# GpSimd adds pairs of probability blocks that only enter softmax sums, so that TensorE weighs one block for two; new planner constants, warm-up and last turn

## What is computed

```python
# layer 0: attention, 16 heads of 8, softmax FIRST, causal mask AFTER it
scores = einsum('bqhd,bkhd->bhqk', Q, K) / sqrt(8)
alpha = softmax(scores, axis=-1)             # sums run over all 1024 keys
alpha = where(causal, alpha, 0)              # then the later keys are dropped
x = x + einsum('bhqk,bkhd->bqhd', alpha, V)
# layers 1 and 3: 8 experts, top 2 by softmax gates (chosen with a bias), and one shared expert
# layer 2: the same attention with rotary tables, no mask, output matrix and bias
```

## Time and profile before

| | us |
|---|---|
| runs shown | 1748.45, 1748.89, 1739.39 |
| median | 1748.45 |
| the profiled execution's own time | 1754.32 |
| its span, first to last instruction | 1752.6 |

### The profile page before, as it was taken

The page is one execution under the profiler, slowest core; times in us unless marked ns, Lnnn a source line. Parts: engine busy times, 40 slices in busy tenths (PEclk is TensorE's granted clock), DMA queues, the critical chain, the costliest instruction groups (busy, mean ns, idle before and its releaser), DMA issues.

```text
span 1752.6 us, 44428 instructions
## 1 busy us (share of the span) xinstructions
PE 1710.3 (98%) x16824; PEld 866.0 (49%) x16824; DVE 1527.3 (87%) x2895; ACT 1420.8 (81%) x2840; POOL 945.8 (54%) x1397
## 2 busy tenths in 40 slices
PE   7999999999999999999999999999999999999988
PEld 3444444555545555455554545445454455555557
DVE  7888888998989989899889999889998989999727
ACT  2688887898878888688886998879997889999862
POOL 5254444566966678476772546535544364555530
PEclk7799998999989999899999999989997999999999
DMA  5211111000101001010110102010110001100000
GB/s 171 89 55 63 69 57 51 21 21 20 57 2 56 21 20 56 12 47 21 32 45 2 38 20 74 20 38 2 45 33 13 2 13 34 38 8 2 8 7 13
DMA packets 39124, 61.13 MB, mean 35 GB/s; under 512 B 5568, under 2 KB 20544, under 8 KB 38784
## 3 DMA queue, kind: packets, MB, share of 16 engines
q1 hardware_dynamic: 38880, 58.28, 10.2%
q10 hardware_dynamic: 32, 0.01, 0.0%
HBM read 29.96 MB, written 27.26 MB: 33 GB/s over the span
## 4 chain that ended last, share of the span: by engine, by line
PE 89%; DVE 6%; ACT 2%; issue 1%; POOL 1%; SPq 1%; DMA 0%; ACTq 0%; DVEq 0%; POOLq 0%
PE ps_sum L1358 29%; PE ps_banks L1324 25%; PE ps_banks L1378 13%; PE ps_banks L1399 8%; PE ps_banks L1299 4%; DVE negmax L1096 3%; PE ps_banks L1259 2%; PE ps_banks L1313 2%; PE ps_banks L1245 1%; PE ps_banks L1266 1%; PE ps_banks L1369 1%; ACT probs L908 1%; SPq L623 1%; PE ps_banks L1281 1%; PE ps_sum L1337 1%
## 5 line engine op out<-in xcount | busy, mean ns | idle before, releaser
L1096 DVE TENSOR_REDUCE negmax<-ps_banks 128x1 f32<-128x512 f32 x2048 | 1296.0, 684 | 151.7 <-PE ps_banks L1299 131.9
L908 ACT ACTIVATE probs<-ps_banks 128x512 f32<-128x512 f32 x2048 | 1099.9, 610 | 184.6 <-PE ps_banks L1324 176.0
L1299 PE MATMUL ps_banks<-kx,qx 24*128 24x512 f32 x2048 | 603.7, 512 | 6.9 <-DVE negmax L1096 2.4
L1324 PE MATMUL ps_banks<-qx,kx 26*128 26x512 f32 x2048 | 557.2, 508 | 5.8 <-ACT probs L908 3.6
L1358 PE MATMUL ps_sum<-probs,vg 128*9 128x256 f32 (+1 forms) x6144 | 425.8, 381 | 2.0 <-ACT sums L915 1.3
L1324 PEld LDWEIGHTS ps_banks<-qx,kx 26*128 26x128 f32 x2048 | 214.6, 186 | 381.5 <-ACT probs L908 129.4
L781 POOL TENSOR_TENSOR hid<-hid,first 128x512 f32<-128x512 f32 x124 | 158.2, 1276 | 210.2 <-DVE hid L1123 123.6
L1299 PEld LDWEIGHTS ps_banks<-kx,qx 24*128 24x128 f32 x2048 | 243.1, 187 | 38.9 <-DVE negmax L1096 17.6
L793 POOL TENSOR_SCALAR scaled<-scaled,gates 128x128 f32<-128x128 f32 x496 | 175.2, 371 | 80.5 <-ACT scaled L965 79.9
L755 POOL TENSOR_TENSOR pdiag<-probs,causal 128x512 f32<-128x512 f32 x128 | 163.3, 1279 | 98.9 <-ACT probs L908 64.4
L1358 PEld LDWEIGHTS ps_sum<-probs,vg 128*9 128x9 f32 x6144 | 129.0, 90 | 163.2 <-issue 71.3
(11 more groups left out here) (121 smaller groups left out, 1383.6 us busy)
## 6 DMA issues: line engine op xcount, KB each, us to landing
qk_rows<-limbs SPq DMA_DIRECT2D x36, 512.0 KB, 3.7
qx<-qk_rows SPq DMA_DIRECT2D x124, 96.0 KB
kx<-qk_rows SPq DMA_DIRECT2D x124, 96.0 KB
qx<-mlimbs SPq DMA_DIRECT2D x508, 2.0 KB
qk_rows<-prod_c SPq DMA_DIRECT2D x8, 512.0 KB, 3.4
qk_rows<-prod_s SPq DMA_DIRECT2D x4, 512.0 KB, 3.0
out_dram<-x SPq DMA_DIRECT2D x8, 256.0 KB, 2.5
x<-in_x SPq DMA_DIRECT2D x3, 512.0 KB, 6.0
```

The costliest lines, as they stand in the source:

```text
L908: act.activation(m.probs[:, blk % PROB_SLOTS, EXP_HEADS[k], :], bank, ACT.Exp, scale=SCALE).then_inc(s.freed[SCALAR], 1)
L1096: dve.tensor_reduce(m.negmax[:, unit // UNITS % 2, half, col:col + 1], bank, AX.X, ALU.max, negate=True).then_inc(s.freed[VECTOR], 1)
L1299: pe.matmul(bank_of(("scores", unit, k)), m.qx[rows, n % SLOTS, tile * P:(tile + 1) * P], m.kx[rows, n % SLOTS, half * CHUNK:(half + 1) * ...
L1324: pe.matmul(bank, m.kx[rows, n % SLOTS, j * P:(j + 1) * P], m.qx[rows, n % SLOTS, half * CHUNK:(half + 1) * CHUNK], start=True, stop=True) ...
```

## The change

Four things are done. First, in layer 0 and half 0, after the exponentials of blocks j = 5 and j = 7, GpSimd adds the block before into this one, in `m.probs`, over 128 partitions by 2048 elements; TensorE then weighs only the odd block, both parts at the second step of the block two later, after waiting for the new semaphore `paired`. The even block isn't weighed. Second, the account's constants for the banks are replaced. Third, `warm` is made of four tiles in place of two, once per step as before in the first two blocks, and it is put also after the even units from 14 to 24 of `begun`. Fourth, the last chunk's items in `ended` stand at fixed units: `turn` after unit 6 in place of 4, `logits` 7 in place of 6, the chain in units 8, 9, 10 in place of 7, 8, 9.

```diff
+WARM_FROM = 14
-READ_AFTER = 90
-WEIGHT = {"exp": (11, 49), "scores": (11, 60), "h1": (85, 100), "h3": (85, 0), "y": (95, 50), "mix": (95, 90),
-          "turn": (50, 80), "q": (95, 100), "k": (95, 100), "v": (95, 100), "direct": (190, 70), "qk": (95, 69), "logits": (95, 20),
-          "oturn": (50, 50), "omix": (100, 50), "maxima": (20, 25), "sums": (55, 50)}
-OTHER_WORK = {"weigh": (55, 0, 0), "copy": (0, 50, 0), "high": (0, 107, 0), "stats": (0, 0, 120), "moments": (0, 0, 60),
-              "combine": (0, 0, 33), "finish": (0, 0, 25), "chain": (0, 0, 20), "product": (0, 0, 69), "write": (0, 0, 70)}
+READ_AFTER = 80
+WEIGHT = {"exp": (11, 49), "scores": (18, 60), "h1": (54, 100), "h3": (85, 0), "y": (57, 50), "mix": (95, 90),
+          "turn": (50, 80), "q": (95, 64), "k": (95, 60), "v": (95, 160), "direct": (300, 110), "qk": (95, 55),
+          "logits": (95, 20), "oturn": (50, 30), "omix": (100, 50), "maxima": (20, 40), "sums": (55, 50)}
+OTHER_WORK = {"weigh": (55, 0, 0), "copy": (0, 50, 0), "high": (0, 107, 0), "stats": (0, 0, 96), "moments": (0, 0, 75),
+              "combine": (0, 0, 33), "finish": (0, 0, 25), "chain": (0, 0, 12), "product": (0, 0, 86), "write": (0, 0, 70)}
+def only_summed(blk):
+    n, half = place(blk // NT)
+    return masked_after(n) and blk % NT >= (half + 1) * CT
...
         items += both[2:]
+        if part and only_summed(blk) and blk % 2:
+            items.append(("pair", blk))
         if part and diagonal(blk):
             items.append(("mask", blk))
         if blk >= WEIGH_LAG:
+            behind = blk - WEIGH_LAG
             between = any(item[0] in BETWEEN for item in side.get(step + 1 - part, []))
-            items += [("weigh", blk - WEIGH_LAG, k) for k in (range(2 * part) if between else (part,))]
+            if not only_summed(behind):
+                items += [("weigh", behind, k) for k in (range(2 * part) if between else (part,))]
+            elif behind % 2 and part:
+                items += [("weigh", behind, k) for k in range(2)]
...
-            items.append(("warm", blk, part))
+            items.append(("warm",))
...
         plan += side.get(unit, []) + scores_of(unit)
+        if unit >= WARM_FROM and unit % 2 == 0:
+            plan.append(("warm",))
...
-    stages = [[("oturn", c)], [("omix", c), ("oadd", c)], [("stats", 3, c), ("moments", 3, c), ("apply", 3, c)],
-              [("turn", 3, c)], [("logits", 3, c)],
-              *([("chain", 3, c, 1, k) for k in range(CHAIN) if k // PART == part] for part in range(-(-CHAIN // PART)))]
-    side = {}
-    for i, stage in enumerate(stages):
-        add_side(side, {1 + i * (late - 1) // len(stages): stage})
+    side = staged(1, (0, ("oturn", c)), (1, ("omix", c)), (1, ("oadd", c)),
+                  (2, ("stats", 3, c)), (2, ("moments", 3, c)), (2, ("apply", 3, c)), (5, ("turn", 3, c)), (6, ("logits", 3, c)),
+                  *((late - 4 + k // PART, ("chain", 3, c, 1, k)) for k in range(CHAIN)))
...
+    def add_pair(blk):
+
+        pool.wait_ge(s.freed[SCALAR], counts.freed("exp", blk, GH - 1) + 1)
+        one, other = (m.probs[:, k % PROB_SLOTS, :, :].rearrange("p h q -> p (h q)") for k in (blk, blk - 1))
+        pool.tensor_tensor(one, one, other, ALU.add).then_inc(s.paired, 1)
...
-    def warm(blk, part):
+    def warm():
         pe.wait_ge(s.acc_cleared, 1)
-        for t in range(2):
+        for t in range(CT):
...
+            if only_summed(blk):
+                pe.wait_ge(s.paired, counts.nth("pair", blk) + 1)
...
         if part:
-            last.then_inc(s.weighed, 1)
+            last.then_inc(s.weighed, 2 if only_summed(blk) else 1)
```

More of the change, by code:

```diff
@@ L299, in ended @@
     late = len(units) - NE
-    assert late > 2
-    stages = [[("oturn", c)], [("omix", c), ("oadd", c)], [("stats", 3, c), ("moments", 3, c), ("apply", 3, c)],
-              [("turn", 3, c)], [("logits", 3, c)],
-              *([("chain", 3, c, 1, k) for k in range(CHAIN) if k // PART == part] for part in range(-(-CHAIN // PART)))]
-    side = {}
-    for i, stage in enumerate(stages):
-        add_side(side, {1 + i * (late - 1) // len(stages): stage})
+    assert late > 10
+    side = staged(1, (0, ("oturn", c)), (1, ("omix", c)), (1, ("oadd", c)),
+                  (2, ("stats", 3, c)), (2, ("moments", 3, c)), (2, ("apply", 3, c)), (5, ("turn", 3, c)), (6, ("logits", 3, c)),
+                  *((late - 4 + k // PART, ("chain", 3, c, 1, k)) for k in range(CHAIN)))
     items += [("h1", done), ("h3", done), ("product", done)]
@@ L515, in signals @@
     s.hidden, s.added, s.mixed = (sem(k) for k in ("hidden", "added", "mixed"))
-    s.weighted = sem("weighted")
+    s.weighted, s.paired = sem("weighted"), sem("paired")
     s.biased = sem("biased")
@@ L835, in pool_program @@
             mask(*of)
+        elif kind == "pair":
+            add_pair(*of)
         elif kind == "apply" and not by_vector(kind, *of):
@@ L1436, in tensor_program @@
         elif kind == "warm":
-            warm(*of)
+            warm()
         elif kind == "fill":
```

## The result

The kernel after takes 1820.78 us (median of 4 runs, 1818.34 to 1830.08), the kernel before 1745.73 in the same job: a ratio of 1.043, 95% interval 1.040 to 1.046. The forecast was 1775, its range ended at 1801. The profiled execution took 1818.34 us, with a span of 1816.4. Between the medians lie 75.1 us, between the two profiled spans 63.8: the profiled execution of the kernel before, 1754.32, was 8.6 us slower than its median here. First the page of after: busy time, the clock in slices, and the engines of the chain that ended last.

A forecast was written before the change was run, and what follows sets the result against it. TensorE was taken as the bound, busy 1710.3 of 1752.6 us. The terms +21.4 + 5 + 3 + 5 + 0 - 3 - 5 = +26.4 on a median of 1748.45 gave 1775 us, range 1742 to 1801.

The forecast's parts named there:

- What goes: Layer 0: 64 weighed blocks become 32, so at most 32 x 0.98 = 31.4 us go, if TensorE never waits.
- the waits: Layer 0: TensorE stands for GpSimd's adds, 25 to 60 us in all, near 7 us singly in spans 14, 22, 30.
- The clock: Behind four or five long waits, work of some 2 us runs at half rate: +5 us, ends 0 and 20.
- The adds: Layer 0: 32 GpSimd adds over 2048 columns, 4.55 us each, 146 us of GpSimd work.
- The count of the spans: Even spans 10 to 30, with expert units: net shifts of +25.4 us, less 4 for bank waits that go, +21.4.
- The rival that GpSimd's adds might be in time: Layer 0: GpSimd is let through earlier, up to 22 of 31.4 us come through, 1718 us; chance 0.12.
- the clock falls and stays down: After each long wait, half rate over 8 us or so, VectorE held: +15 and +6 more, 1796 us; chance 0.18.
- Spans without expert units: Five spans of layer 0: count gives +10.8 us, half taken because TensorE had slack, +5, ends 0 and 11.
- VectorE's holds: Spans 10, 18 and 26: GpSimd's adds hold up VectorE's chain steps, about 1 us each, +3, ends 0 and 14.
- Account: Bank choice, the only part touching layer 2: 0, ends -12 and +12; layer 2 moving over 10 us would count against the forecast.
- warm-up: At the start: more matmuls may bring the full clock rate earlier, up to -9, or cost +7; taken as -3 us.
- last turn: At the end: the 4.01 us wait for xn goes, and the slow matmuls behind it: -5 us, ends -6 and 0.

The follow-up runs named there:

- e3: The kernel after without GpSimd's adds and the wait for them, the even block of each pair not weighed: 1774.94 us, 1.014 against before.
- e2: The kernel after without the pairs (new bank account, warm-up and last turn kept, every block weighed): 1743.68 us, 1.000 against before.
- e8: The kernel after with each GpSimd add over only half of the pair's columns (1024): 1783.48 us, 1.019 against before.
- e10: The kernel after, complete, plus one fill (0.98 us of zero matmuls) where each even block was weighed: 1822.63 us, 1.040 against before.
- e15: e2 without the added warm matmuls, so with the warm-up of before: 1744.19 us, 0.999 against before.
- e1: The kernel before with the pairs alone (old bank account, warm-up and last turn): 1811.54 us, 1.037 against before.
- e16: The kernel before with the new last turn alone: 1741.31 us, 0.997 against before.
- e6: e2 with two fills of zero matmuls added per former pair, all weighings kept: 1807.97 us, 1.033 against before.
- e9: e3 with one fill of zero matmuls in place of each weighing left out: 1764.57 us, 1.008 against before.

## Why the forecast missed

Two steps failed. "What goes" put 31.4 us of TensorE's work down as time, of which under 3 came; the waits were counted too long by about as much, so that this error hardly shows in the total. The clock, put at +5, cost about 55 (an estimate, below): that is the term that took the time out of the range.

**The adds, right.** 4.53 us against 4.55; GpSimd's busy time up by 143.8 (forecast 146); in spans 14, 22 and 30 the second add starts 5.23 to 5.24 us after its data (5.4). The list between the adds is what the forecast said.

**"What goes", wrong: the step that failed first.** "TensorE is the bound there", from 99.89 of 100 busy, and so at most 31.4 us go. e3 less e2 shows under 3 us. The count of the spans then set the saved 0.98 against each wait. Rows 2 can't show a bank wait that matmuls in flight cover, and VectorE at 90.90 and ScalarE at 85.89 in that same row were the warning: three engines pass the same banks on to each other, and each bounds the others. The rival that GpSimd's adds might be in time, priced at 1718, would not have come out there even if it had been true: e8 is nearly that case, with 3.6 us of waits, and takes 1783.

**The waits, too long, and right in the net by luck.** Measured 22.8 us in 13 waits, the longest 5.3, against 25 to 60 with some near 7. Of them 15.1 fall in the spans with expert units; the count's gross waits there were 25.4 and the 22 x 0.98 it had taken off, 47. So there the waits were 32 us too long, and the saving nearly 22 too large. TensorE comes later to each wait than I had it: it saves nothing on the way, and ahead of the long wait in span 14 it was at the half rate. The net looks right because the two errors nearly cancel: after less e2, the line through the 32 spans has a slope of 0.35 and crosses zero at +0.77; the 157 us more at the half rate make 55 us of the 79.5, and the rest is 24.5, where the forecast had 21.4 and 5 for the same waits. The split is rough: the crossing has a standard error of 11 us over the 32 spans, and e10 shows that clock and waits stand in for each other. The long waits' spans do cost more than the forecast's +5.5: spans 14 and 15 together 8.2 us over e2, 22 and 23 7.3, 30 and 31 8.3, with 10.2, 6.8 and 13.7 us more at the half rate.

**The clock, wrong in kind and size.** +5 against about 55 (an estimate, from the slope above). The forecast let the clock fall behind the long waits only, and for some 2 us. In after, layer 0 has 18 stretches at the half rate, of 3.4 to 20.5 us, and some stand behind gaps of under 0.5 us: e3, where TensorE waits for no add, and e8, where it waits 3.6 us, have 109 and 106 us of layer 0 at the half rate, e2 17. Of the rivals, "the clock falls and stays down" had the direction; with its 15 us more it had 20 for the clock, over a third of what came. The Trainium skill (TensorE: Matmul & The Clock Gate, "Terms") prices throttled time at half of it; here the slope is a third, 0.31 to 0.35, as if part of a half-rate stretch were hidden behind the other engines, which is not shown by itself. By the skill's half the 157 us would be 79 (an estimate from that page), the whole of the change, and nothing would be left for the waits.

**Spans without expert units, wrong by the clock.** +5 against +29.3 (after less e2, spans 0 to 9). Their half-rate time rose by 77 us, which at 0.35 is 27; the remaining 2 is near the forecast, though 7.7 us of the waits stand there. I had called the 4 us of idle time in 100 slack. It was where the clock is nearest to its fall (0.95 in rows 2).

**VectorE's holds, the mechanism right, off the path.** The three chain steps of spans 10, 18 and 26 fell into the adds, 2294 ns for the longest of a group whose median is 208:

```profile
L1212 DVE TENSOR_TENSOR room<-rank,small x20: 179/208/2294, 341.6 to 1792.3; 128x64 f32<-128x64 f32 x12, 128x32 f32<-128x32 f32 x8
```

In spans 18 and 26 the time against e2 rose by 0.5 and 0.3 us. So of +3 most did not come.

**Account, warm-up, last turn.** The account was put at 0: e2 and e15 are at 1.000 and 0.999, so no change can be told from it. Layer 2, which only the account touches, is 9.6 us shorter in after, just short of the 10 that were to count against the forecast. That is not the account: e1, with the account of before, has 803.5 too. Over the 17 profiles with the new account, layer 2 takes 0.30 us more for each us that it has at the half rate (13.7 to 61.4 us), and none lies over 2.3 us off that line; it gives 811.2 at the 47.8 us of before and 804.0 at e1's 23.9, where 810.2 and 803.5 were measured. So the account moves layer 2 by about 1 us. The line bears out the third of a us with no pairs near. The warm-up was put at -3: the start is 5.3 us longer, and over the twelve profiles with this warm-up and full maxima it takes 51.3 to 56.1 us, against 46.1 to 48.6 in the four with the old one. The last turn was put at -5, and the end is 5.8 us shorter in after, e2 and e16 alike: the transpose of after no longer waits, and takes 0.60 us instead of 0.66 behind 4.01 us of waiting:

```profile
1776.43 0.60 PE L1265 MATMUL ps_banks<-ident,xn 128*128 128x128 f32 x4
```

**The sum.** The forecast was +26.4. Measured is +63.8 in the span: of the missing 37.4, the clock is +50 (an estimate, 55 for 5) and the start +8.3; the shorter layer 2 gives back 9.6, e2's shorter layer 0 (824.9 for 830.5) 5.6, the holds 3, the waits 1.9 and the end 0.8. The 9.6 and the 5.6 go with less time at the half rate, 13.7 us for 47.8 and 17.1 for 56.7, and the profiled execution of before was a slow one: by medians the miss is 11 us larger than this sum.

## What to carry to other kernels

Before counting a removed piece of work as time, look at what stands behind it in that engine's order: if the next item needs a buffer that a nearly saturated neighbour must free, the removed piece was filling the wait. Three engines at 100, 91 and 86 of 100 acted here as one bound, not as one bound and two followers. And work taken from TensorE can lower its clock and so cost more than it saved: read the granted clock per stretch as a term of the sum, at about a third of a us for each us at the half rate here.

## What the hardware showed unexpectedly

- Work taken away lowered the clock: half-rate time of layer 0 from 17.1 us (e2) to 109.2 (e3), with no gap above 0.48 us in the stretch ahead of the fall looked at.
- Asymmetry: 63 us of added matmuls cost 59.8 us (e6), 31.4 us of removed ones gained less than 3 (e3), and 31 us put back cost 9 (e9), each apart from the clock.
- e9 has the TensorE time of e2, with a fill of zeros for each weighing left out, and still 54.6 us at the half rate against 17.1. Why fills hold the clock less well than the weighings is open.
- With the same work, layer 2 took 800.6 to 815.4 us in single executions, and its time followed its half-rate time by 0.30 us per us.
